# The last addition of the second layer's channel mixture, computed by GpSimd instead of VectorE

## The reference, cut to what matters

```
xc  = _ln(x, ln2_w, ln2_b)
sxc = concatenate([state, xc[:, :-1]]) - xc
rr  = sigmoid((xc + sxc * fmaa_r) @ fWr.T)
kk  = square(relu((xc + sxc * fmaa_k) @ fWk.T))
x   = x + rr * (kk @ fWv.T)          # the addition of this line is the one that moves
```

## Time and profile before

| | |
|---|---|
| median of 3 runs | 3607.91 us (3607.87 to 3610.71) |
| the profiled execution | 3604.68 us, of which its span 3602.7 us |
| TensorE busy | 3384.8 us (94%) |
| VectorE busy | 2357.3 us (65%) |
| ScalarE busy | 1713.6 us (48%) |
| GpSimd busy | 191.9 us (5%) |
| granted TensorE clock, mean | 0.966 of full speed |
| the addition that moves (L1731) | 8 times, 1226 ns each, from 1692.2 to 2345.7 us |

### The profile page before, as it was taken

One profiled execution on the slowest core, in us unless ns is written; L12 is line 12 of the kernel. 1 busy time (PEld: TensorE's weight loads), 2 busy tenths in 40 slices (PEclk: granted clock), 3 DMA queues, 4 the chain that ended last, 5 costly groups with the idle time before them and its releaser, 6 DMA issues. The chain is left out here.

```text
span 3602.7 us, 53141 instructions
## 1 busy us (share of the span) xinstructions
PE 3384.8 (94%) x20600; PEld 2490.7 (69%) x20600; DVE 2357.3 (65%) x3723; ACT 1713.6 (48%) x4121; POOL 191.9 (5%) x311
## 2 busy tenths in 40 slices
PE   7999999999999995889999998779999999699998
PEld 6777788878887784556666665456666666488885
DVE  5666665666666663599999999446777777542212
ACT  4445444544444443445556554336666666532222
POOL 0000000000000000000000000011001111000000
PEclk9999999999999997889999999889999999899999
DMA  4333212221121113344444444040000000120004
GB/s 176 119 116 130 106 71 88 101 95 71 71 106 71 71 71 141 82 112 103 109 112 103 109 106 104 25 155 7 1 22 21 30 16 16 68 70 24 24 12 159
DMA packets 88952, 287.57 MB, mean 80 GB/s; under 512 B 19744, under 2 KB 27936, under 8 KB 64128
## 3 DMA queue, kind: packets, MB, share of 16 engines
q1 hardware_dynamic: 62576, 182.28, 17.2%
q0 software_dynamic: 10368, 75.50, 5.6%
q10 hardware_dynamic: 15760, 26.40, 2.1%
HBM read 229.63 MB, written 54.53 MB: 79 GB/s over the span
## 5 line engine op out<-in xcount | busy, mean ns | idle before, releaser
L453 ACT ACTIVATE l_prob<-l_bank,l_nmax 128x512 f32<-128x512 f32 x512 | 344.9, 686 | 280.7 <-DVE l_nmax L539 280.7
L539 DVE TENSOR_REDUCE l_nmax<-l_bank 128x1 f32<-128x512 f32 x512 | 317.6, 683 | 68.9 <-PE l_bank L373 68.9
L339 PE MATMUL l_bank<-l_x_hi,l_w_hi 128*128 128x256 f32 x1024 | 296.8, 290 | 15.9 <-DVE l_x_lo L598 15.9
L339 PE MATMUL l_bank<-l_x_hi,l_w_lo 128*128 128x256 f32 x1024 | 289.9, 283 | 0.0
L339 PE MATMUL l_bank<-l_x_lo,l_w_hi 128*128 128x256 f32 x1024 | 289.7, 283 | 0.0
L562 DVE COPY l_probT<-l_bank 128x512 f32<-128x512 f32 x256 | 173.7, 689 | 175.8 <-PE l_bank L387 174.8
L1611 DVE TENSOR_TENSOR_SCAN l_kv<-l_wx,l_kv 128x2056 f32<-128x2056 f32 x64 | 283.8, 4435 | 1.9 <-DVE l_nrs L1624 1.6
L2122 ACT ACTIVATE l2a_sc<-l2a_sc,l2a_nmax 128x256 f32<-128x256 f32 x512 | 254.0, 515 | 27.8 <-DVE l2a_nmax L2192 27.8
L387 PE MATMUL l_bank<-l_ident,l_prob 128*128 128x128 f32 x2048 | 249.3, 277 | 15.2 <-DVE l_k_lo L555 10.6
L387 PEld LDWEIGHTS l_bank<-l_ident,l_prob 128*128 128x128 f32 x2048 | 227.2, 142 | 28.9 <-DVE l_k_lo L555 20.8
L409 PE MATMUL l_bank<-l_probT,l_v 128*64 128x512 f32 x1024 | 233.8, 598 | 0.0
(11 more groups left out here) (290 smaller groups left out, 7625.7 us busy)
## 6 DMA issues: line engine op xcount, KB each, us to landing
l_vb<-vd SPq DMA_DIRECT2D x64, 1024.0 KB
l_w_hi<-kept_w_hi POOLq DMA_DIRECT2D x24, 1024.0 KB, 8.1
l_w_lo<-kept_w_lo POOLq DMA_DIRECT2D x24, 1024.0 KB, 10.1
l_wv_hi<-kept_wv_hi POOLq DMA_DIRECT2D x12, 1024.0 KB, 5.1
l_wv_lo<-kept_wv_lo POOLq DMA_DIRECT2D x12, 1024.0 KB, 7.1
l_wraw<-in_l_wqk SPq DMA_DIRECT2D x8, 1024.0 KB, 8.4
kept_w_hi<-l_w_hi SPq DMA_DIRECT2D x8, 1024.0 KB, 10.8
kept_w_lo<-l_w_lo SPq DMA_DIRECT2D x8, 1024.0 KB, 12.4
```

The costliest lines, as they stand in the source:

```text
L339: mm = pe.matmul(s.ap[:, c * ROWS:(c + 1) * ROWS], a[:, kt, c, g, :], b[:, kt, c * ROWS:(c + 1) * ROWS], start=m == 0, stop=m == 3 * KT - 1)
L453: act.activation(prob[h][:, it, :], s.ap[:, :], ACT.Exp, bias=nmax[:, n % 2, it, h:h + 1], accum_out=rsum[:, n % 2, it, h:h + 1]).then_inc ...
L539: dve.tensor_reduce(nmax[:, n % 2, it, h:h + 1], s.ap[:, :], AX.X, ALU.max, negate=True).then_inc(max_ready, 1)
```

## The change

The addition leaves `out_part` of VectorE. GpSimd gets a helper `add_out(c)` which waits until both halves of `rv_ready` of batch c are there, adds, and raises `out_ready` as before. It stands at the beginning of GpSimd's step c+2, ahead of that step's `csd`; the last one stands behind the loop. The repeated constants lower in the file change nothing.

```diff
+                def add_out(c):
+                    pool.wait_ge(rv_ready, 2 * c + 2)
+                    pool.tensor_tensor(xres[:, :, :], xres[:, :, :], tmp_rows, ALU.add).then_inc(out_ready, 1)
+
                 for b in ALL:
+                    if b >= 2:
+                        add_out(b - 2)
                     if b >= 1:
                         deviations(csd, cdev_in, cdev_ready, b - 1)
                     if b + 2 < B:
                         pool.wait_ge(nvar_ready, b + 3)
                         pool.tensor_tensor(nrs[:, :], nrs[:, :], power[:, :], ALU.pow).then_inc(nrs_ready, 1)
                         deviations(sd, dev_in, dev_ready, b + 2)
+                add_out(B - 1)
...
                     for half in H2:
                         dve.wait_ge(rv_ready, 2 * c + half + 1)
                         dve.sem_inc(S[f"fv{c}_{half}"].drained, 1)
-                    dve.tensor_tensor(xres[:, :, :], xres[:, :, :], tmp_rows, ALU.add).then_inc(out_ready, 1)
```

More of the change, by code:

```diff
@@ L1780, in _ @@
                             out_part(c)
+NH, HD = 16, 32
+QUAD = P // HD
 NH, HD = 16, 32
```

## The result

The changed kernel takes 3613.74 us (median of 22 runs, 3608.50 to 3620.58), beside 3608.53 us for the kernel before (22 runs, 3601.18 to 3614.05). The ratio is 1.0017, with a 95% interval of 1.0011 to 1.0024, so the addition on GpSimd costs 6.1 us (4.0 to 8.7). The forecast was 4.9 us over the 3607.91 us shown. That is within 0.2% of no change, though clearly not zero.

A forecast was written before the change was run, and what follows sets the result against it. TensorE and VectorE both nearly full; TensorE and ScalarE set the time from fv to L1649, VectorE after. Terms 1.84 + 1.00 + 1.00 + 1.04 = 4.88 us, added to the median 3607.91, gave 3612.8 us; range 3605.0 to 3618.0.

The forecast's parts named there:

- What VectorE gains: Behind the second L1727: without the addition the scan starts sooner, 1.29 - 0.24 = 1.05 us per addition if nothing else happened.
- What GpSimd's addition does: Behind out_part: GpSimd starts before the scan and holds VectorE's two-input SBUF reads for 2.21 us, making VectorE 1.00 us later.
- The four steps with time to spare: Batches 0, 2, 3, 4: of 1.00 us, 0.54 is spare at L1649, so 0.46 gets through; 4 x 0.46 = 1.84 us.
- step 3: Batch 1: ScalarE was done before VectorE came to L1649, so nothing to spare; the full 1.00 us is lost.
- rival 1: VectorE sets the pace everywhere, each of six additions costing its full price: 7.0 to 7.8 us slower; chance 20%.
- TensorE's wait for L1656: TensorE's wait at L1041 for VectorE's L1649 (L1656 after the change) would grow from 0.39 to about 0.85 us.
- Batch 5: Step 7: no idle time behind the addition and no later VectorE wait on another engine; costs 1.00 us.
- Batch 6: GpSimd ends at 2285.45 us, ScalarE's L1416 starts at 2285.77: 0.3 us to spare, VectorE idle, cost 0.
- rival 5: The clock falls otherwise: each fall costs 1.7 us on TensorE, plus or minus 1.7 to 3.4 us on any case; 12%.
- Batch 7: The layer's last addition: GpSimd would end at 2347.99 us instead of 2346.95, 1.04 us later at the layer's end.
- No hold (2 and 3): GpSimd does not hold VectorE: spare time eats the gain, 3607.4 us, 11%; or VectorE sets the pace, 3602.6 us, 5%.
- Starving (4): GpSimd gets in only at VectorE's idle 0.54 us; five steps lose about 9.6 us each, +48 us; chance 2%.

The follow-up runs named there:

- write-only kernel: Changed kernel with GpSimd filling the same tile with ones by memset, reading nothing and not computing the addition; 0.9983 of the kernel before, -6.1 us.
- the second of the last pair: Kernel before, except GpSimd adds from an own tile a step later in halves, beside VectorE work with two SBUF inputs; last batch on VectorE; ratio 1.0025.

## Why the prediction was right, and where it was not

- **What VectorE gains.** Forecast 1.05 us with no hold. The write-only kernel starts the instruction behind the scan 4.61 us after the mark instead of 5.64: 1.03 us. Right.
- **What GpSimd's addition does.** Forecast: a start 0.08 us behind the multiplication, 2.34 us long, GpSimd ahead of the scan, VectorE held and 1.00 us late. Measured: 0.08, 2.35, ahead of it, 2.06 us on the scan's record, 1.02 us late. The twin of another layer, L2192 beside the same addition, gave the price to 0.02 us. The Trainium skill ("SBUF — State Buffer", section "Who interferes with whom") has VectorE instructions with two SBUF inputs and GpSimd's reads exclude each other, and lets a GpSimd write pass. The held scan and the free memset agree. Its lock for the whole instruction would make VectorE 1.13 us late; the 1.02 us measured say that it is let go some 0.1 us before the recorded end.
- **The four steps with time to spare, and step 3.** Forecast 4 x 0.46 + 1.00 = 2.84 us, measured 3.31 us as a difference of means whose members scatter by 5 us. The price of a step came out as forecast: 0.39 us in the steps where L1649 waited for ScalarE, 0.89 to 1.02 us in the others, beside 0.46 and 1.00. How many steps wait did not: 8 of 15, and not 4 of 5. At these prices the 15 steps have a mean of 0.66 us, 3.3 us for five. I had one profile with four waiting steps in five; another execution of the same kernel had one. The 0.54 us to spare were not the kernel's: they stand only behind a slow product with fWr. In the other steps rival 1, VectorE sets the pace, is the right description. That 3.31 lies so near 2.84 is in part luck, as the profiles of the changed kernel have four slow products ahead of these marks and those of the kernel before have eight.
- **TensorE's wait for L1656.** Forecast 0.85 us, measured 5.8, 5.8 and 7.4 us in five steps, 1.2 to 1.5 us each on average. Before it was 2.4, 4.4 and 3.0 us, 0.5 to 0.9. The growth of about 0.6 us is near the forecast 0.46; the level of 0.39 that I added it to is that of the slow steps.
- **Batch 5.** Forecast 1.00, measured 1.29 us. Right within the scatter.
- **Batch 6, a wait that was read wrongly.** Forecast 0, since ScalarE's squares came 0.3 us after GpSimd's end. Instead ScalarE waits for GpSimd 1.17, 0.8 and 0.9 us in the three profiles. The cover had been read from the kernel before. In the changed one VectorE, and so the start of GpSimd's addition, is later in step 7 (1.29 us from mark to mark), and TensorE's product for the squares is late by less (0.70 us in the mean): had I taken my own 1.00 us off, the 0.3 us of cover would have become -0.7. My own term for batch 5 said that this delay was 1.00 us; I didn't carry it into the next line.
- **What that wait costs, and what lies behind mark 6.** The wait is not the 1.04 us of the table. Counted from mark 6, the squares start at 2.51, 2.52 and 2.51 us in the changed kernel and at 2.74, 2.03 and 2.71 us before: 0.02 us later in the mean. What the wait does is to hand on VectorE's lateness, which the term of batch 5 already holds. Counted from mark 5 the squares are 1.31 us later (86.31 against 85.00), where batches 5 and 6 together were forecast at 1.00. The rest of the way to mark 7 took 59.80, 59.38 and 59.81 us before and 61.20, 59.25 and 61.60 us changed, 1.02 us more, and there TensorE's product with Wo differs. In the first pair its rows, before and changed, and the stretches with the columns of the earlier trace rows are:

```profile
2298.15 8.83 PE L1021 MATMUL l_bank<-l_w_Wo,l_y 128*128 128x512 f32 x16 [2.65 <-DVE l_y L1695]
2308.24 9.88 PE L1028 MATMUL l_bank<-l_w_Wo,l_y 128*128 128x512 f32 x16 [2.66 <-DVE l_y L1702]
```

```profile
2298.15:2306.98 8.83, 8.83 (x16) 3.53 (x16) 0.69 (x1) 0.00 (x0) 0.00 (x0) 0.81 0.00 0
2308.24:2318.12 9.88, 9.88 (x16) 4.04 (x16) 0.69 (x1) 0.00 (x0) 0.00 (x0) 0.72 0.00 0
```

The granted clock over it was 0.81 before and 0.72 changed. In the other profiles the product took 8.83 us twice before, and 8.58 and 10.15 us changed. So this is the mechanism of rival 5, the clock. Whether the change brings it about isn't shown: the product took 9.74 to 10.03 us in the three other kernels in which VectorE was made later (both with the addition twice, and the second of the last pair), and 8.83 us in the five others.
- **Batch 7.** Forecast 1.04, measured 1.04 us in all three pairs. Where nothing lies beside the moved work and nothing can catch up, a sum of rows was exact.
- **Rivals.** No hold (2 and 3): out, by the scan's 6.49 us. Starving (4): out, no addition took over 2.36 us, though with a second one behind it 6.37 us are seen. Clock (5): real, and not the same on both sides: it goes with the 5.5 us between two executions of one kernel, and with the 1.02 us behind mark 6. How much of the timed 6.1 us it is stays open.

The terms make 4.9 us and the parts measured 6.7, timed 6.1: 1.04 of the 1.8 us between lie behind mark 6, where TensorE's product was slower, 0.47 us in the five full steps and 0.29 us behind batch 5.

## What to carry to other kernels

Moving an elementwise fp32 operation with two SBUF inputs from VectorE to GpSimd cost VectorE about twice what it saved (2.06 us held against 1.03 us saved for 128x1024) where what followed there also read two SBUF tensors; put it beside instructions that read PSUM or have one input, or leave it. A cover read from the old profile has to be lessened by the delay that the change makes upstream of it. And a spare time of half a microsecond can belong to an execution and not to the kernel: look whether the other engine's work in that step ran at its usual length, and take a second profile before counting steps by it. Last, a wait that appears in the changed kernel isn't yet a cost: compare the same instruction's time from a common mark before laying a sum at its door.

## What the hardware showed that was not expected

- VectorE's instructions follow each other without a gap in the records, and GpSimd still gets in between two of them: its second addition waited for the running scan only, and the half of the last kernel for the running L1630 only (3.19 us). I had a rival in which it waits for VectorE's next idle time.
- An engine's record grows while it stands still: the same instruction is 4.43 or 6.49 us "busy". So VectorE's busy share (98.4 and 97.8% of a stretch) hid the whole effect of the change.
- GpSimd's memset of 128x1024 takes 0.95 us beside a scan of 4.44 us, with neither slowed.
- One kernel's layer scatters by 5.5 us between executions on one core, with the product with fWr at 7.13 us or at 8.5 to 10.05 us. Beyond 7.13 us these products took 6.2, 1.4 and 6.2 us more between marks 0 and 7 in the three profiles of the kernel before, so their durations alone could make 4.8 of the 5.5 us; no run tests it.
